# A graph network's weight matrix in DRAM: tile-major rows, or slices of rows

## The reference

```python
edge_index = jnp.stack([src, dst])
h = jnp.maximum(_layernorm(x, axis=-1), 0.0)
x = x + _L0_gnn_ref(h, edge_index, L0_gnn_W, L0_gnn_b)           # GCN, by out-degree
...
x = x + _L1_gnn_ref(h, src, dst, L1_gnn_Wq, L1_gnn_Wk, L1_gnn_Wv)  # attention, 4 heads
...
x = x + _L2_gnn_ref(h, edge_index, edge_weight, ...)             # two weighted layers
...
x = x + _L3_gnn_ref(h, edge_index, edge_attr_16, ...)            # messages by edge attributes
```

```python
msg = x[src] * ew[:, None]
agg = jax.ops.segment_sum(msg, dst, num_segments=n)
agg = agg + x
neigh = agg / cnt[:, None]
out = x @ Ws.T + bs + neigh @ Wn.T + bn + bias
return jnp.where(out > 0, out, NEG_SLOPE * out)
```

## Time and profile before

| | us |
|---|---|
| median of 3 runs | 2923.5 |
| lowest, highest | 2922.21, 2934.07 |
| span of the profiled execution | 2789.0 |

### The profile page before, as it was taken

How to read it: one execution, slowest core, us unless ns; L and a number is a source line. 1 busy time by engine, 2 the same in 40 slices (tenths; PEclk the granted TensorE clock), 3 DMA queues, 4 the chain that set the end, 5 groups by cost and what they waited for, 6 DMA issues and landing times. The chain is left out here.

```text
span 2789.0 us, 65350 instructions
## 1 busy us (share of the span) xinstructions
PE 2275.2 (82%) x23024; PEld 1658.8 (59%) x23024; DVE 1811.8 (65%) x3137; ACT 1459.7 (52%) x2773; POOL 1889.4 (68%) x1286
## 2 busy tenths in 40 slices
PE   4577777774974888888888888778997999999998
PEld 3466666662432555555656566533544788888887
DVE  8799999994344776777777776411113666666665
ACT  0498989983025888888888887100002333223222
POOL 3487878831506877777787775277775787888884
PEclk7699999996985999999999999899997999999999
DMA  2366767666803111111111112898693332222223
GB/s 52 113 178 189 193 193 196 188 187 186 206 23 88 50 49 49 49 49 49 49 49 49 49 49 16 185 220 189 123 219 72 72 61 59 58 60 56 60 53 60
DMA packets 241964, 285.30 MB, mean 102 GB/s; under 512 B 162714, under 2 KB 180451, under 8 KB 238566
## 3 DMA queue, kind: packets, MB, share of 16 engines
q1 hardware_dynamic: 193035, 248.38, 36.0%
q0 software_dynamic: 48784, 35.00, 6.6%
HBM read 170.23 MB, written 112.10 MB: 101 GB/s over the span
## 5 line engine op out<-in xcount | busy, mean ns | idle before, releaser
L384 POOL DMA_INDIRECT scratch_slots<-sort_pay,sort_slot x440 | 638.8, 1452 | 201.3 <-issue 200.3
L1908 POOL TENSOR_TENSOR score<-score,rise 125x1000 f32<-125x1000 f32 x261 | 559.2, 2162 | 234.3 <-DVE peaks L1850 193.5
L2283 POOL DMA_INDIRECT gathered_rows<-scratch_projected,src_i x385 | 474.0, 1231 | 125.4 <-issue 116.8
L1850 DVE CUSTOM_DVE_ANT_0 score<-raw,log_in 125x1000 f32<-125x1000 f32 (+1 forms) x348 | 330.4, 969 | 177.4 <-PE raw L1707 104.5
L1727 PE MATMUL probsT<-ident,score 125*125 125x125 f32 x2175 | 352.2, 292 | 25.8 <-ACT score L1784 14.8
L1774 ACT ACTIVATE rise<-raw 125x1000 f32<-125x1000 f32 (+1 forms) x350 | 312.7, 918 | 114.0 <-PE raw L1707 75.9
L1727 PEld LDWEIGHTS probsT<-ident,score 125*125 125x125 f32 x2175 | 293.1, 198 | 104.4 <-DVE weighed L1864 56.7
L861 PE MATMUL built<-pair_weight,hot 125*128 125x125 bf16 x3750 | 247.1, 227 | 86.4 <-DVE pair_weight L806 85.1
L861 PEld LDWEIGHTS built<-pair_weight,hot 125*128 125x128 bf16 x3750 | 225.2, 103 | 103.4 <-DVE pair_weight L806 102.1
L1707 PE MATMUL raw<-QT,key 32*125 32x500 f32 x1200 | 182.7, 678 | 93.9 <-DVE peaks L1850 88.4
L1864 DVE COPY weighed<-probsT 125x500 f32<-125x500 f32 x400 | 250.0, 671 | 13.2 <-PE probsT L1727 12.7
(11 more groups left out here) (305 smaller groups left out, 4341.2 us busy)
## 6 DMA issues: line engine op xcount, KB each, us to landing
weights_in<-scratch_weightsT SPq DMA_DIRECT2D x50, 1093.8 KB
scratch_weightsT<-wT SPq DMA_DIRECT2D x25, 1367.2 KB
scratch_logs<-log SPq DMA_DIRECT2D x75, 437.5 KB
log_in<-scratch_logs SPq DMA_DIRECT2D x75, 437.5 KB
counts_in<-scratch_counts SPq DMA_DIRECT2D x25, 683.6 KB
scratch_counts<-cc SPq DMA_DIRECT2D x24, 683.6 KB
scratch_slots<-sort_pay,sort_slot POOLq DMA_INDIRECT x440
weights_in<-scratch_weightsT SPq DMA_DIRECT2D x50, 127.0 KB
```

What stands on the lines that cost most here:

```text
L384: nc.gpsimd.indirect_dma_start(rows, bass.IndirectOffsetOnAxis(ap=slot[:, c:c + 1], axis=0), pay[:, c, :], None).then_inc(sort["placed"][u ...
L1850: nc.vector.tensor_tensor_reduce(out=halves(score[u][h]), in0=seen, in1=halves(log_in[:]), scale=1.0, scalar=FLOOR, op0=ALU.add, op1=ALU.m ...
L1908: nc.gpsimd.tensor_tensor(score[u][h][:, here], score[u][h][:, here], rise[:, b, PIECE * (1 - k):PIECE * (2 - k)], ALU.add).then_inc(added, 1)
L2283: nc.gpsimd.indirect_dma_start(gathered[:, g % GATHERS, k, :], None, projected, bass.IndirectOffsetOnAxis(ap=src_i[:, FIRST + g, k:k + 1], ...
```

## The change

The DRAM tensor `weightsT` gets the order slice, row, tile, column. What one fetch needs, four neighbouring tiles of one slice, is then 4 x 625 contiguous floats in each row: 125 runs of 10,000 bytes instead of 500 of 2500. The store of a tile in the adjacency writes five runs of 2500 bytes per row where it wrote one of 12,500. The general path stores its blocks of weights to the new places. No transfer is added or taken away, and no wait or buffer in SBUF changes.

```diff
@@ adjacency, SyncE
                 sp.wait_ge(copied, t * (2 * NGRP) + (4 + 2 * NGRP))
-                start_rows(sp, row(weightsT, t), wT[:, u, :], stored[u])
+                start_rows(sp, weightsT[:, :, bass.ds(t, 1), :].rearrange("s p o c -> p (s o) c"),
+                           wT[:, u, :].rearrange("p (s c) -> p s c", s=TILES // SLICE), stored[u])
@@ general_adjacency
-            with nc.Fori(0, TILES) as a:
+            with nc.Fori(0, TILES // SLICE) as part, nc.Fori(0, SLICE) as place:
+                a = part * SLICE + place
...
-                            for k, out in enumerate((logs, weightsT, counts)):
+                            for k, out in ((0, logs), (2, counts)):
                                 sp.dma_start(out[bass.ds(t, 1), :, bass.ds(a * P, P)].rearrange("o p n -> (o p) n"),
                                              made_blocks[:, k, :]).then_inc(stored, 16)
+                            sp.dma_start(weightsT[bass.ds(part, 1), :, bass.ds(t, 1), bass.ds(place * P, P)].rearrange(
+                                "s p o n -> (s p) (o n)"), made_blocks[:, 1, :]).then_inc(stored, 16)
@@ fetch_weight_slice
-    per = TILES // SLICE
     slot = chunk % SLOTS2
-    cols = slice((chunk % per) * SLICE * P, (chunk % per + 1) * SLICE * P)
-    start_rows(sp, ring[:, slot, 0:n, :], weightsT[first:first + n, :, cols].rearrange("t p c -> p t c"), loaded[slot])
+    start_rows(sp, ring[:, slot, 0:n, :], weightsT[chunk % (TILES // SLICE), :, first:first + n, :], loaded[slot])
@@ program
-    weightsT = dram("scratch_weightsT", (TILES, P, N), F32)
+    weightsT = dram("scratch_weightsT", (TILES // SLICE, P, TILES, SLICE * P), F32)
```

More of the change, by code:

```diff
@@ L47 @@
 WEIGHED = 2 * GRP - 1
+GROUP = 4
+SLICE = 5
 BATCHES = 11
@@ L1940, in _ @@
             link(nc.vector.reciprocal(per_node[:], per_node[:]))
-GROUP = 4
-SLICE = 5
 SLOTS2 = 2 * (TILES // SLICE)
```

## The result

The changed kernel took **2939.28 us** (median of 20 runs, 2929.44 to 2958.16) where the kernel before, on the same chip, took 2921.01 (20 runs, 2906.11 to 2943.98): a ratio of **1.0061**, 95% interval 1.004 to 1.0081, or 18 us more. The forecast was 2927 with a range of 2913 to 2943, 3.5 us above the kernel before. The time lies in the range and on the forecast's side, but the loss is five times the one forecast: the kernel became slower by more than 0.5%, for which the chance given was 0.11 to 0.13.

The account below looks back on a forecast made before the run. GpSimd's scatter chain was taken to bound the weighted layers by under 2 us: -43 us on TensorE hidden, +4 on GpSimd's first load, 0 in the adjacency, giving 2793 in the span and 2927 us, range 2913 to 2943.

Parts of the forecast that it names:

- Step 1: Weight fetches in the weighted layers: 10,000-byte runs move 290 GB/s instead of 223, so a slice takes 4.3 us, not 5.6.
- TensorE's 43 us: In the weighted layers, TensorE would end some 43 us earlier through faster fetches, near 2086 us.
- The first rival: Weight fetches stay at 223 GB/s whatever the run, TensorE and the first load end as now: 2923 us, chance 0.12.
- GpSimd covers the gain, and bounds the stage by under 2 us: In the weighted layers, GpSimd's scatter chain already ends last, by under 2 us, and hides TensorE's whole 43 us gain.
- Step 2: GpSimd's load of its first batch in the weighted layers lands later: +4 us on its chain, from -8 to +17.
- the one of turns: GpSimd's first load takes turns with single weight runs, each 552 ns instead of 180: at most 16.8 us later.
- The gaps: GpSimd's pauses ahead of a batch's last scatter, 7.70 and 7.00 us, taken as unchanged, with 1 us each in the range.
- The third rival: GpSimd's transfers wait behind 10,000-byte runs: 2940 us for the load alone, up to 2960 if scatters fall behind; chance 0.16.
- Step 3: Adjacency stores of 625 runs of 2500 bytes per tile instead of 125 of 12,500: cost zero, bounds 0 and 33 us.
- The sum: Whole kernel: span 2789.0 us becomes 2793, plus 134.5 us around it taken as unchanged, gives 2927 us.

Follow-up runs that it names:

- before_again: The kernel before, unchanged, profiled once more beside the others as a single execution: 2798.53 us, its stage of the weighted layers 393.9 us.
- the second pair: The kernel before and the changed kernel, both unchanged, run again in one comparison on one chip: ratio 1.0084.
- half_runs: The changed kernel with one unused float behind every second tile in the ring, so fetches are 250 runs of 5000 bytes: ratio 0.9993 to the kernel before.
- short_runs: The changed kernel with one unused float behind each tile in the ring, so fetches are again 500 runs of 2500 bytes: ratio 1.0011 to the kernel before.
- after_packed_first: The changed kernel with the attributes of all five batches loaded and packed before the stage's first scatter: ratio 1.0095 to the kernel before.
- after_one_semaphore: after_packed_first with all 200 scatters of the stage raising the same semaphore instead of alternating between two: ratio 1.0083 to the kernel before.

## Why the prediction was right or wrong

**Step 1, the faster reads: wrong, and the first error.** It divided a rate by the share of busy time in a stretch where the engines were not full, 199 GB/s at 0.73, called the quotient (273) the rate of 6250-byte runs, and drew a line on to 290 at 10,000. The share can't be divided out: reads of those same rows move 227 GB/s, not 273, where the engines are full. The trace of before had that stretch, and I hadn't read it, 680 to 690 us, where they start:

```profile
680.00:690.00 10.00, 2.71 (x8) 1.09 (x9) 3.27 (x13) 0.00 (x0) 5.32 (x7) 0.50 1.02 227
```

One stretch of 10 us is no exact rate: the same one shows 235 to 256 GB/s in the other traces, at shares of 1.01 to 1.03. None reaches 273. What settles it is the pair without scatters, 229 GB/s with 2500 bytes and 224 with 10,000. So step 1 should have had no gain, and TensorE's 43 us never existed. The objection named ahead, the rule of the Trainium skill ("DMA: Bandwidth & Descriptors", Why small descriptors are slow) that merging gains little above 256 bytes, has the trace on its side: 224 GB/s against 229 is not even its 4 per cent. The first rival, "the reads don't get faster", held as far as it goes, and its time (2923) didn't, since it left GpSimd as it was.

**GpSimd covers the gain, and bounds the stage by under 2 us: half right.** Its chain does end last after the change, and VectorE's idle time there is the line that shows it. But the margin of one execution isn't that of the kernel: before_again had 10 us of slack on GpSimd. In that pair the slack is why 33 us on GpSimd's chain became 21 us of stage.

**Step 2, the first load: right direction, size short, mechanism not settled.** +4 us was forecast within -8 to +17; it measured +7.0 and, in the second pair, +6.5. Of its two limits the one of turns had the right sign, and there was no faster stream to free the load. half_runs (+2.8 us at 5000 bytes) and short_runs (13.5 us) tie it to the length of a run. The Trainium skill ("DMA: Bandwidth & Descriptors", Queues, rings and completion order) has each DMA engine go round between the queues, changing only after a whole packet of descriptors. By that a queue with longer descriptors holds the engine longer; the load's landing agrees in direction, and the gaps, unmoved at 5000 bytes, do not follow it in proportion. Nor does the load where it is issued one block earlier, 19.89 us beside 2500 bytes and 13.41 beside 10,000: the order holds only at the place where the load stands in the two kernels.

**The gaps, "I take these as they are": the step that decided.** It put 1 us on each, because the gap of 7.00 us at 1995.93 came "where fetches have only begun again". But the share from 1988 to 1996 us was 0.79 already, at 202 GB/s; and where the engines have less to do the gap is 2.3 to 3.3 us (2.29 was in the earlier trace rows, at the end), so it does depend on the transfers. Having both in view, I should have carried a bound for it. It measured +23.3 us of the 30.3.

**The third rival was the one that came, by another road.** "Long runs hold GpSimd back" was given 2940 to 2960 and a chance of 0.16. Its price was right at the lower end: 2939. Its reasoning was not: it had each scatter pass several long runs and fall behind its interval of 1.5 us. The scatters between gaps kept their 1.49 us; the loss sits in one place in forty, and in the first load.

**Step 3, the stores: right.** short_runs has them all and stands at 1.0011. After, the stretch 400 to 440 us has a share of 0.69 and VectorE busy 38.57 us, where the earlier trace rows had 0.71 and 38.71.

**The sum: a wrong base that did no harm.** It took 134.5 us as lying around the span. A run lies 2 us above its span (2942.5 and 2940.5 for the profiled execution of after); the rest would be the edge stage at a lower clock in the timed runs, as in the profile of after, where it takes 767.6 us and not 640.6. As it was added to both sides, the forecast of the difference wasn't touched.

Two small slips in step 1 change nothing: seven scatters in 10 us at a share of 0.10 are 0.57 us for four, not 0.45, and five groups of 7.9 us are 39.5, not 39.6.

So the number is luck in part: the time fell into the range because the range had room for the load in turns, while 23.3 of the 30.3 us came from the gaps. Of the chances, some 0.8 on "no difference" was too much for an argument that left the largest term at a value of its own choosing.

## What to carry to other kernels

Read a transfer's rate only from stretches where the DMA share is about 1, and compare run lengths there; runs of 2500, 5000 and 10,000 bytes moved the same 200 to 250 GB/s in the stretches read here, so longer runs are no reason for a new layout. Before making one queue's transfers coarser, look at which other queue shares the DMA engines with it and whether that engine's chain is near the end of the stage: each of its waits that is longer under load is a term of the sum, also one that the profile calls "issue". When two chains end within a few microseconds of each other, profile a second time before saying which one bounds.

## What the runs showed that I had not expected

- GpSimd stalls after 39 scatters in a row on one semaphore: 2.3 us with the DMA engines nearly idle, 7.4 to 8.7 in saturation beside runs of 2500 or 5000 bytes, up to 21.4 beside 10,000 when loads go between the scatters. It needs no wait or copy of the program, and 385 gathers that change semaphore every five have none. That the semaphore is what counts fits every trace and is not tested.
- Runs of 10,000 bytes are no faster than runs of 2500 (224 and 229 GB/s alone on the engines, 210 and 208 to 216 beside scatters), but GpSimd waits 19.6 us for its first load beside them instead of 13.1 (16.3 beside 5000 bytes). Issued one block earlier, the load does not follow this order.
- GpSimd's 200 scatters and five loads cost TensorE's chain 34 to 43 us in this stage, where they run beside the fetches. The two share no data in it, only the DMA engines: without them the fetches move 229 GB/s for 216, and TensorE's wait for the matrix falls from 35.0 to 8.0 us. Where the scatters start only after all five loads have landed, the same work costs it 9 and 20 us (345.8 in after_packed_first and 356.9 in after_one_semaphore against 336.7).
- The same program ran at 2793 to 2921 us on different chips. Between the trace ahead of the prediction and that of after, it is the clock in the edge stage that differs, 1.00 and 0.87.
